# Four GNN layers on one core: the build of the pair matrices without its loop, second one-hots dealt out anew

## What is computed

```python
coef = comp[etypes]                          # 8 relations, 4 bases
m = coef[:, 0, None] * hb[0][src]            # hb[b] = h @ basis[b]
for b in range(1, 4):
    m = m + coef[:, b, None] * hb[b][src]
agg = segment_sum(m * norm[:, None], dst)    # norm: edge_weight
out = agg + bias + h @ loop_w                # twice, comp0/basis0 and comp1/basis1
```

## Time and profile before

| | us |
|---|---|
| median of 3 runs (2359.51 to 2361.01) | 2360.82 |
| profiled execution, its own time | 2358.45 |
| its span in the trace | 2356.7 |
| PE busy over the span | 2050.9 (87%) |
| DVE busy | 1805.9 (77%) |
| ACT busy | 1422.6 (60%) |
| POOL busy | 1261.7 (54%) |

### The profile page before, as it was taken

How to read it: one execution, slowest core, us unless ns; L and a number is a source line. 1 busy time by engine, 2 the same in 40 slices (tenths; PEclk the granted TensorE clock), 3 DMA queues, 4 the chain that set the end, 5 groups by cost and what they waited for, 6 DMA issues and landing times. The chain is left out here.

```text
span 2356.7 us, 37537 instructions
## 1 busy us (share of the span) xinstructions
PE 2050.9 (87%) x11455; PEld 1104.7 (47%) x11455; DVE 1805.9 (77%) x3754; ACT 1422.6 (60%) x2254; POOL 1261.7 (54%) x1066
## 2 busy tenths in 40 slices
PE   0687688789988949999999987999999999999965
PEld 0433577546655624444444453455555454555422
DVE  7999799853333349999999873899999999999723
ACT  1898777511112214444444433899999999999822
POOL 2575577508720033333333203688888887888530
PEclk9998899989999969999999999999999999999988
DMA  2410100102143344333333404332222222222000
GB/s 113 163 28 13 55 0 0 58 28 79 41 110 99 88 141 140 91 91 91 91 92 95 87 1 124 90 97 74 80 76 70 76 76 71 77 74 79 10 0 22
DMA packets 81566, 170.36 MB, mean 72 GB/s; under 512 B 17378, under 2 KB 43221, under 8 KB 80449
## 3 DMA queue, kind: packets, MB, share of 16 engines
q0 software_dynamic: 35840, 98.88, 15.6%
q1 hardware_dynamic: 45624, 70.25, 9.1%
HBM read 144.93 MB, written 23.98 MB: 72 GB/s over the span
## 5 line engine op out<-in xcount | busy, mean ns | idle before, releaser
L896 PE MATMUL e_two_ps<-w,e_first 128*128 128x512 bf16 x1408 | 420.0, 380 | 0.1
L655 POOL DMA_INDIRECT sorted_records<-edge_record,slot_row x160 | 209.8, 1311 | 126.4 <-POOLq L796 58.0
L896 PE MATMUL e_two_ps<-w,e_first_low 128*128 128x512 bf16 x704 | 267.3, 380 | 0.0
L1790 POOL TENSOR_TENSOR e_first_low<-e_first 128x1024 bf16<-128x1024 f32 x88 | 250.1, 2842 | 21.9 <-DVE e_first L1981 21.9
L1795 POOL TENSOR_TENSOR e_msg_low<-e_act 128x1024 bf16<-128x1024 f32 x88 | 225.5, 2563 | 56.2 <-DVE e_act L1993 54.9
L1627 ACT ACTIVATE u_msg<-u_t,slot_record 128x128 f32<-128x128 f32 x528 | 172.9, 391 | 97.4 <-DVE u_t L1666 88.2
L2286 POOL DMA_INDIRECT e_got<-src_table,e_idx x176 | 186.7, 1061 | 70.5 <-issue 35.7
L1546 POOL DMA_INDIRECT u_got<-up_table,u_idx x176 | 168.5, 957 | 76.8 <-issue 43.7
L896 PEld LDWEIGHTS e_two_ps<-w,e_first 128*128 128x128 bf16 x1408 | 134.5, 98 | 148.6 <-issue 2.2
L1592 PE MATMUL u_sum_ps<-u_msg,u_hot 128*125 128x512 f32 x352 | 189.7, 621 | 14.9 <-DVE u_msg L1683 11.7
L697 PE MATMUL pairs_ps<-cell_high,src_hot 128*128 128x144 bf16 x1180 | 153.7, 227 | 49.6 <-POOL cell_rest L721 27.5
(11 more groups left out here) (368 smaller groups left out, 5218.5 us busy)
## 6 DMA issues: line engine op xcount, KB each, us to landing
conv_w<-in_L_gnn_basis_dram SPq DMA_DIRECT2D x8, 1024.0 KB
sorted_records<-pairs SPq DMA_DIRECT2D x5, 1408.0 KB, 11.1
edge_record<-in_edge_floats_dram SPq DMA_DIRECT2D x2, 3125.0 KB
later_w<-in_L_gnn_W_dram SPq DMA_DIRECT2D x6, 1024.0 KB
attr_parts<-h SPq DMA_DIRECT2D x22, 256.0 KB, 2.1
e_attrT<-attr_parts SPq DMA_DIRECT2D x44, 128.0 KB
e_dst_all<-dst_row SPq DMA_DIRECT2D x44, 125.0 KB
pairs<-in_edge_floats_dram SPq DMA_DIRECT2D x1, 3125.0 KB
```

What stands on the lines that cost most here:

```text
L655: pg.nc.gpsimd.indirect_dma_start(out=pg.sorted, out_offset=bass.IndirectOffsetOnAxis(ap=pg.slot_row[:, j:j + 1], axis=0), in_=pg.edge_rec ...
L896: last = nc.tensor.matmul(out, lhsT, rhs, start=(n == 0), stop=(n == len(pairs) - 1))
L1790: nc.gpsimd.tensor_tensor(first_low[:, r % 2, 2 * u:2 * u + 2, :], full, upper(full), ALU.subtract).then_inc(low1, 1)
```

## The change

The three loops over items and POOL's loop become plain Python loops, so all 118 items stand in the program one after the other, with constants for semaphore values and offsets. The second one-hot is DVE's in items 7, 15, ..., 111 (`g % 8 == 7`), 14 items, and ACT's in the other 104; before it was DVE's in 29 and ACT's in 89. `made_by_act(g)` counts ACT's items before g.

```diff
-    ROUND, DVE_TURN = 4, 3
+    ROUND = 8
+    def by_dve(g):
+        return g % ROUND == ROUND - 1
+    def made_by_act(g):
+        return g - g // ROUND
...
-            def products(g, h, turn, second):
+            def products(g, h):
...
-                    elif turn != DVE_TURN:
-                        pe.wait_ge(second_hot, second)
+                    elif not by_dve(g):
+                        pe.wait_ge(second_hot, made_by_act(g) + 2)
...
-            with pe.Fori(0, (NI - 2) // ROUND) as i:
-                for turn in range(ROUND):
-                    products(ROUND * i + turn, turn % 2, turn, DVE_TURN * i + turn + 2)
-            for turn in range(2):
-                products(NI - 2 + turn, turn, turn, DVE_TURN * (NI - 2) // ROUND + turn + 2)
+            for g in range(NI):
+                products(g, g % 2)
...
-            with pool.Fori(0, NI // 2) as i:
+            for i in range(NI // 2):
...
-            with act.Fori(0, (NI - 2) // ROUND) as i:
-                for turn in range(DVE_TURN):
-                    operand(ROUND * i + turn, turn % 2, DVE_TURN * i + turn + 1)
-            for turn in range(2):
-                operand(NI - 2 + turn, turn, DVE_TURN * (NI - 2) // ROUND + turn + 1)
+            for g in range(NI):
+                if not by_dve(g):
+                    operand(g, g % 2, made_by_act(g) + 1)
...
-                for k in range(2 if turn == DVE_TURN else 1):
+                for k in range(2 if by_dve(g) else 1):
...
-            operand(0, 0, 0)
-            with dve.Fori(0, (NI - 2) // ROUND) as i:
-                for h in range(ROUND):
-                    operand(ROUND * i + h + 1, (h + 1) % 2, (h + 1) % ROUND)
-                    add(ROUND * i + h, h % 2)
-            operand(NI - 1, 1, 1)
-            add(NI - 2, 0)
-            add(NI - 1, 1)
+            operand(0, 0)
+            for g in range(NI):
+                if g + 1 < NI:
+                    operand(g + 1, (g + 1) % 2)
+                add(g, g % 2)
```

More of the change, by code:

```diff
@@ L752, in _, with operand @@
         def _(dve):
-            def operand(g, h, turn):
+            def operand(g, h):
                 dve.wait_ge(used, g + 1)
-                for k in range(2 if turn == DVE_TURN else 1):
+                for k in range(2 if by_dve(g) else 1):
                     last = nc.vector.tensor_scalar(src_hot[:, h, k, :], names,
```

## The result

| | before | after |
|---|---|---|
| median of 7 runs each (us) | 2360.77 (2359.51 to 2361.80) | 2354.86 (2351.98 to 2356.18) |
| profiled execution, its own time | 2358.45 | 2354.86 |
| its span | 2356.7 | 2352.9 |
| ACT's last copy in the stage ends | 449.77 | 443.23 |
| span behind that | 1906.9 | 1909.7 |

The ratio is 0.9975, with a 95% interval from 0.9964 to 0.9986: 5.9 us less. The forecast was 2354.9, also 5.9 us less. ACT's last copy ends 6.5 us earlier, and in the profiled execution 2.7 us of that were gone at the end of the span.

What follows compares the result with a forecast made beforehand. A closed chain of add, one-hots and PE through the odd items was taken as the bound; -6.9 + 1.0 = -5.9 us gave 2352.55 profiled, 2354.9 as median. Range 2352.5 to 2363, about 0.8.

Steps and rivals of the forecast that it cites:

- The chain: Middle of the stage: DVE's add, DVE's one-hots, then PE, through the odd items, set the period, 6.44 us per four items.
- links of 2.99 and 3.45 us: From PE's end of one odd item to the next: 2.99 us with one DVE one-hot, 3.45 with two.
- ACT's step: Between ACT's two dependent functions per item: 0.87 us without the loop; rival that ACT becomes the bound, 2372 us, chance 0.09.
- the two straight items: Items 116 and 117, already outside the loop before; ACT's step between them was 0.87 us, against 0.98 inside the loop.
- the narrow place of the forecast: ACT's first to second function, unseen unhindered in straight code: 0.87 us taken; at 0.96 ACT bounds, gaining 0.07 per eight items.
- Fifteen double one-hots fewer: Odd items where DVE makes both one-hots, 29 to 14: each removed saves 0.46 us, 6.9 us in all.
- The end of the stage: After item 115: ACT makes all last second one-hots, so the last ends 1.9 us after it instead of 0.93; cost 1.0.
- loop counters and registers: Loop counters and register operations in the stage go; counted as 0 us.
- Branches and code loads: PE's removed branches, 0 (far bound 6 us); about 20 code loads, 0; rival that PE waits for code, 2381 us, chance 0.10.
- the short link: Odd item to odd item with one DVE one-hot, 2.99 us; POOL's product gets earlier there, DVE doesn't, so 0 gained.

Runs made afterwards that it cites:

- straight4: The kernel before with only the loops made straight, DVE still making the second one-hot of one item in four: ratio to before 1.0032.
- even8: The changed kernel with DVE's 14 second one-hots at items 6, 14, 22, ..., all even: ratio to before 0.9974.
- parity: The changed kernel with DVE's 14 second one-hots at items 7 and 14 of every sixteen, alternating odd and even: ratio to before 0.9963.
- act3: The changed kernel with three scratch tiles for ACT, its first function issued an item ahead, and all second one-hots on ACT: ratio to before 0.9948.
- deep8: The changed kernel with three ACT scratch tiles, a third buffer for one-hots and cells, and DVE's one-hots made two items ahead: 2328.3 us, ratio to before 0.9866.
- loop8: The kernel before with loops kept, turns of eight items, the last six straight, DVE making one second one-hot in eight: ratio to before 1.0034.
- straight16: The changed kernel with DVE making only one second one-hot in sixteen: ratio to before 1.0004.

## Why the prediction was right, and where it was off

**The chain.** Right, and exact: links of 2.99 and 3.45 us, 24.84 per sixteen items (2 x 12.42 forecast). `straight4`, `even8`, `parity`, `act3` and `deep8` each move one part of it, and the period followed: 25.76 with the old share, 23.93 with none, 21.28 with the one-hots out of it.

**ACT's step.** Right. The value taken from the two straight items was 0.87; it measured 0.86 for both steps. The one that wasn't seen before, first to second function, was the narrow place of the forecast: at 0.96 the gain would have been nothing. `loop8` shows that case, `straight16` shows ACT as the bound at 1.72.

**Sizes.** Fifteen double one-hots fewer gave 6.9 us, as reckoned. The end of the stage cost 0.9 (1.0 forecast): the last one-hot ends at 438.50 + 0.83 = 439.33. Left out was the beginning. The first add starts at 258.5 instead of 259.0 us. Of these 0.5 us, 0.3 come from ahead of the stage and are chance, since the code there is the same. The other 0.2 are the start without loops: the first add comes 5.5 us after the last operation of the stage before in all ten profiles without loops, and 5.75 in all three with them. I had priced loop counters and registers at 0. So the stage gained 6.9 + 0.2 - 0.9 = 6.2 instead of 5.9 us, and its end moved by 6.5.

**The hit in the total** is partly luck. The 6.5 us at the end of the stage met medians that differ by 5.9, and the time behind the stage, which I took as fixed, differs by 1 us between the two profiles of the changed kernel and by 6 between those of the kernel before. On one chip, 22 runs of the kernel before lie between 2353.9 and 2365.3 us. The range covered that only because it was widened for other reasons.

**Branches and code loads.** 0 for both was right: 19 loads (20 forecast) with no idle time, also at 1.33 us per item. Removing 29 branches of PE gave nothing in the period of `straight4`.

**POOL** is earlier in the short link, as expected: its product ends 0.19 us before the one-hot (302.19 against 302.38), where it ended with it before. It is worth nothing, since DVE is as late as it was.

**What I didn't think of** is that a version of this edit can lose 7 us in a layer 1000 us later. It happened to `straight4`, not to the change (in neither of its two profiles). A rival "the edge layer falls into its other pattern" belonged into the list, with 7 us as its price.

## What to carry to other kernels

Follow one period of a software pipeline link by link; if the links close on the period, what counts is which items carry the extra work, not how much work an engine has. Loads can then be moved to a busier engine up to the point where its own step times its share reaches the chain's period, and buffers that take an operation out of the chain were worth more here than either. Judge a change of a few us by its own stage in the profile, and look at what the rest of the kernel does in a second profile before the total is explained.

## What the runs showed of the hardware

An ACT function that waits for ACT's previous one starts 0.03 us after its end where the wait is a constant (0.06 in a few), and 0.11 to 0.16 us after it where the value comes from a register of the loop (steps of 0.86 against 0.94 to 0.99 at a duration of 0.83). Over an item that was 0.2 us, enough to turn a gain of about 6 us into a loss of 7.

A DVE operation of 128x1024 that meets POOL's subtraction doesn't slow down evenly: it took 2.90 us instead of 1.23 and ended 1.08 us after POOL's, and 79 others in that profile ended at the same distance, however long POOL's still ran. The Trainium skill's "SBUF — State Buffer", section "SBUF: two separate sides", says that the two engines share a pair of ports which whoever starts first holds for its whole instruction, if the DVE operation has two inputs in SBUF and POOL's reads SBUF, as L1976 and L1796 do. The trace agrees with that: the extra 1.67 us are close to the 1.82 us for which POOL's instruction still ran, and the 1.08 us that follow it are nearly the whole 1.23 of an undisturbed operation.

Copies of one program differed by up to 6 us in time behind the stage, with the clock's stretches at the lower level in different places.
